# Layer 1 self-attention hands its output over by features instead of by tokens, and the dense stage behind it reads it so

## The reference

```
q = fq_sym(x @ Wq); k = fq_sym(ctx @ Wk); v = fq_sym(ctx @ Wv)     # 20 heads of 16
scores = einsum('bhnd,bhmd->bhnm', q, k) * dh ** (-0.5)
w = fq_zero(softmax(scores, axis=-1))                              # rounded to 255 levels of one global step
out = einsum('bhnm,bhmd->bhnd', w, v).transpose(0, 2, 1, 3).reshape(b, n, c)
return out @ Wo + bo
```

## Time and profile before

| what | value |
| --- | --- |
| median of 3 runs | 3719.68 us (3715.29 to 3727.21) |
| profiled execution, its own time | 3716.17 us |
| its span, first to last instruction | 3714.4 us |
| layer 1 self-attention, second block, start of the first to start of the last exponential | 2266.1 to 2564.3 us |
| the dense stage behind it | 2571.7 to about 2757 us |
| PE, DVE, ACT, POOL busy over the span | 80%, 62%, 52%, 19% |

### The profile page before, as it was taken

How to read it: one execution, slowest core, us unless ns; L and a number is a source line. 1 busy time by engine, 2 the same in 40 slices (tenths; PEclk the granted TensorE clock), 3 DMA queues, 4 the chain that set the end, 5 groups by cost and what they waited for, 6 DMA issues and landing times. The chain is left out here.

```text
span 3714.4 us, 51380 instructions
## 1 busy us (share of the span) xinstructions
PE 2975.6 (80%) x16324; PEld 1854.4 (50%) x16324; DVE 2303.9 (62%) x4118; ACT 1916.2 (52%) x3264; POOL 724.2 (19%) x1076
## 2 busy tenths in 40 slices
PE   5989999776969999979599996897750217699999
PEld 3744444464548888858111111223640104488888
DVE  4668888465533444346699996886653866344443
ACT  3438888532533323235599997996322325232322
POOL 1021111334440000000453511002330205300000
PEclk8979999887989999989555555666975559799999
DMA  6643333244730000015765436672324103201000
GB/s 182 208 143 105 104 108 105 63 117 127 184 88 18 9 17 8 0 57 153 175 156 115 114 63 88 79 98 48 89 75 152 28 11 73 45 17 32 16 23 15
DMA packets 477771, 307.04 MB, mean 83 GB/s; under 512 B 304150, under 2 KB 415982, under 8 KB 476942
## 3 DMA queue, kind: packets, MB, share of 16 engines
q1 hardware_dynamic: 471230, 288.64, 33.0%
q0 software_dynamic: 4240, 14.10, 1.3%
q10 hardware_dynamic: 2112, 1.97, 0.3%
HBM read 183.70 MB, written 118.78 MB: 81 GB/s over the span
## 5 line engine op out<-in xcount | busy, mean ns | idle before, releaser
L2053 DVE TENSOR_REDUCE neg_max<-nat 128x1 f32<-128x512 f32 x640 | 400.7, 682 | 65.0 <-PE nat L1919 64.9
L2248 PE MATMUL nat<-k_stack,q_stack 48*128 48x512 bf16 x640 | 380.7, 604 | 71.5 <-DMA k_stack<-k1w 30.8
L2282 DVE TENSOR_REDUCE m_all<-nat 128x1 f32<-128x512 f32 x640 | 423.3, 690 | 17.4 <-PE nat L2248 17.1
L2302 ACT ACTIVATE nat<-nat,m_all 128x512 f32<-128x512 f32 x640 | 427.7, 2129 | 2.3 <-DVE m_all L2282 2.3
L2302 ACT ACTIVATION_READ_ACCUMULATOR nat<-nat,m_all 128x1 f32 x640 | 403.7, 1674 | 0.0
L937 DVE SCALAR_TENSOR_TENSOR ff<-outp,bias,gel 128x512 f32<-128x512 f32 x160 | 120.1, 751 | 427.8 <-PE outp L407 427.8
L1992 ACT ACTIVATE probs<-sT 128x1024 f32<-128x1024 f32 x320 | 327.9, 1026 | 89.9 <-PE sT L1928 80.3
L2479 ACT ACTIVATE exps<-sT 128x1024 f32<-128x1024 f32 x320 | 296.3, 1083 | 15.6 <-PE sT L2419 13.7
L868 ACT ACTIVATE gel<-outp,bias 128x512 f32<-128x512 f32 x160 | 110.0, 687 | 360.6 <-PE outp L407 360.6
L749 POOL TENSOR_TENSOR rstd<-var_eps,neghalf 128x4 f32<-128x4 f32 x48 | 49.2, 1025 | 1147.6 <-DVE var_eps L919 1147.5
L872 ACT CAST ff_hi<-ff 128x512 fp32r<-128x512 f32 x160 | 99.2, 620 | 312.0 <-DVE ff L937 312.0
(11 more groups left out here) (444 smaller groups left out, 7000.5 us busy)
## 6 DMA issues: line engine op xcount, KB each, us to landing
v<-vpad SPq DMA_DIRECT2D x64, 320.0 KB, 2.8
q_stack<-q_part SPq DMA_DIRECT2D x90, 160.0 KB, 5.8
k_stack<-k1w SPq DMA_DIRECT2D x90, 160.0 KB, 10.6
q_stack<-q_hi SPq DMA_DIRECT2D x160, 64.0 KB, 2.5
k_stack<-k_hi SPq DMA_DIRECT2D x160, 64.0 KB, 2.2
v_stack<-v SPq DMA_DIRECT2D x40, 256.0 KB, 3.1
self_out<-o_nat SPq DMA_DIRECT2D x80, 128.0 KB, 2.0
attn_nat<-self_out SPq DMA_DIRECT2D x64, 160.0 KB, 2.9
```

The source lines that it names most:

```text
L2053: dve.tensor_reduce(neg_max[:, n % 2, qt, 2 * pr + ab:2 * pr + ab + 1], nat[(16 * (n + 2) + t) % 3][:, :], AX.X, ALU.max, negate=True).the ...
L2248: pe.matmul(bank[i % NAT][:, :], q_stack[half, slot, g, pr, qt * P:(qt + 1) * P], k_stack[half, slot, g, pr, :], start=True, stop=True).th ...
L2282: dve.tensor_reduce(k.m_all[:, column(i // TILES, i % TILES)], bank[i % NAT][:, :], AX.X, ALU.max, negate=True).then_inc(s["e_max_ready"], 1)
L2302: act.activation(b[:, :], b[:, :], ACT.Exp, bias=k.m_all[:, col], accum_out=k.s_all[:, col]).then_inc(s["a_nat_free"], 1)
```

## The change

The attention output stays as it lies in the bank: DVE scales o_ps straight into o_sb (two slots), SP stores the 16 rows of each of four heads by a DMA of its own, 2 KB per row, to self_out_T with features as rows. The transposes, the copy and o_nat go. The dense stage loads feature rows into attn_T by three DMAs and splits them from there: oT keeps its ACT and DVE steps, and loses PE's transposes and their banks. SP's next load waits until all three splits of the sample before are done (oT_split).

```diff
 def dense_phase(..., next_weights=(), by_feature=False):
+            attn = sb("attn_T", [P, 3, TOK]) if by_feature else sb("attn_nat", [P, TT, ZCOL])
+            n_attn = 3 if by_feature else TT + 1
 # SP
+                def load_attn_T(b, split_b=None):
+                    if split_b is not None:
+                        sp.wait_ge(s["oT_split"], at["oT_split"] + split_b * 3 + 3)
+                    src = rows(attn_in, b * D, D)
+                    sp.dma_start(attn[:, 0:2, :], src[0:2 * P].rearrange("(c p) t -> p c t", p=P)
+                                 ).then_inc(s["attn_in_loaded"], 16)
+                    for half in range(2):
+                        sp.dma_start(attn[64 * half:64 * half + 64, 2, :], src[2 * P:D]).then_inc(s["attn_in_loaded"], 16)
 # PE
-                    if kind == "oT":
+                    if kind == "oT" and not by_feature:
 # ACT (and DVE's subtraction likewise)
-                        act.copy(oT_hi[:, m, :], bank_of(st, r)[:, :]).then_inc(s["oT_hi_done"], 1)
+                        src = attn[:, m, :] if by_feature else bank_of(st, r)[:, :]
+                        act.copy(oT_hi[:, m, :], src).then_inc(s["oT_hi_done"], 1)
 def exact_self_attention
-            o_sb = sb("o_sb", [P, TOK], own=own)
-            o_nat = sb("o_nat", [P, 2, TT, 4, DH], own=own)
+            o_sb = sb("o_sb", [P, 2, TOK], own=own)
 # SP
-                            wait(sp, "a_o_normed", n - 1)
-                            sp.dma_start(rows(out, (n - 2) * TOK, TOK).rearrange("(t p) c -> p t c", p=P),
-                                         o_nat[:, n % 2].rearrange("p t h c -> p t (h c)")
-                                         ).then_inc(s[f"a_o_stored{n % 2}"], 16)
+                            wait(sp, "a_o_scaled", n - 1)
+                            for h in range(4):
+                                sp.dma_start(rows(out, (n - 2) * 64 + h * DH, DH), o_sb[VCOL * h:VCOL * h + DH, n % 2, :]
+                                             ).then_inc(s[f"a_o_stored{n % 2}"], 16)
 # PE
-                    for u in range(NU + UNITS + 1):
+                    for u in range(NU + LAG + 1):
-                        if u % UNITS == 0 and u >= 2 * UNITS:
-                            turn_output(u // UNITS - 2)
 # DVE
+                    def scale_output(n):
+                        wait(dve, "a_pv_done", TT * (n + 1))
+                        if n >= 2:
+                            wait(dve, f"a_o_stored{n % 2}", 64 * (n // 2))
+                        dve.tensor_scalar(o_sb[:, n % 2, :], o_ps[n % 2][:, :], k.out_step, None, ALU.mult
+                                          ).then_inc(s["a_o_scaled"], 1)
-                        if j == 3 and 1 <= n <= NQ:
-                            copy_output(n - 1)
-                        if j == 1 and n >= 2:
-                            norm_output(n - 2)
+                        if j == 6 and 1 <= n <= NQ:
+                            scale_output(n - 1)
```

More of the change, by code:

```diff
@@ L549, in dense_phase @@
         if main == "ff":
-            turned = {st: ("misc", n, 10) for n, st in enumerate(oT + oproj + zT)}
+            turns = ([] if by_feature else oT) + oproj + zT
+            turned = {st: ("misc", n, len(turns)) for n, st in enumerate(turns)}
         else:
             turned = {st: (st[0], st[1], n) for n, part in ((3, oT), (TT, oproj), (3, zT)) for st in part}
+            if by_feature:
+                turned = {st: x for st, x in turned.items() if st[0] != "oT"}
             if not has_o:
@@ L846, in step @@
                     if kind == "oT":
-                        bank_full(act, st, b)
+                        if not by_feature:
+                            bank_full(act, st, b)
+                        elif m == 0:
+                            act.wait_ge(s["attn_in_loaded"],
+                                        at["attn_in_loaded"] + b * (16 * n_attn) + 16 * n_attn)
                         if m == 0:
@@ L901, in step @@
                         dve.wait_ge(s["oT_hi_done"], at["oT_hi_done"] + b * 3 + m + 1)
-                        dve.tensor_tensor(oT_lo[:, m, :], bank_of(st, r)[:, :], oT_hi[:, m, :].bitcast(F32),
-                                          ALU.subtract).then_inc(s[turned[st][0] + "_drained"], 1)
+                        src = attn[:, m, :] if by_feature else bank_of(st, r)[:, :]
+                        done = "oT_split" if by_feature else turned[st][0] + "_drained"
+                        dve.tensor_tensor(oT_lo[:, m, :], src, oT_hi[:, m, :].bitcast(F32), ALU.subtract
+                                          ).then_inc(s[done], 1)
                     elif kind == "oproj":
@@ L2118, in exact_self_attention @@
             **{f"a_v_loaded{r}": 16 * BATCH // 2 for r in range(2)},
-            **{f"a_o_stored{r}": 16 * NQ // 2 for r in range(2)}}
+            **{f"a_o_stored{r}": 64 * NQ // 2 for r in range(2)}}
         at = {name: s.before(name) for name in counts}
@@ L2428, in products @@
                             if n >= 2:
-                                wait(pe, "a_o_normed", n - 1)
+                                wait(pe, "a_o_scaled", n - 1)
                         wait(pe, "e_rounded", u + 1)
@@ L2436, in products @@
                         mm.then_inc(s["a_pv_done"], 1)
-                    def turn_output(n):
-                        wait(pe, "a_o_copied", n + 1)
-                        for qt in range(TT):
-                            mm = pe.transpose(o_ps[n % 2][:, qt * P:(qt + 1) * P], o_sb[:, qt * P:(qt + 1) * P],
-                                              k.ident[:, :])
-                        mm.then_inc(s["a_o_turned"], 1)
                     wait(pe, "a_recip", 1)
```

47 lines of the change are left out of this document (22 added, 25 removed).

## The result

The changed kernel takes 3740.97 us in the median of 4 runs (3739.7 to 3745.43), the one before 3720.69 beside it (3715.29 to 3727.21): the ratio is 1.0056, 95% interval 1.0038 to 1.0074. It is slower, by about 20 us where 9 were forecast. It lies 1 us inside the range of 3711 to 3742, and outside the 3719 to 3739 that the prediction gave for its own mechanism. The profiled execution has a span of 3739.0 us.

What follows compares the result with a forecast made beforehand. Bounds: ACT's exponentials in attention, POOL's bias additions at the dense start, then a chain through z and hT_lo. 3716.17 - 5 + 15 - 3.4 + 5 = 3727.8, put at 3729 towards the runs' higher median; range 3711 to 3742.

Steps and rivals of the forecast that it cites:

- The turnings: Attention: without the transposes and copy per quad, ACT gets its scores sooner; -5 us (4 to 6).
- The late store: Attention: six scalings wait 3.2 us for a store behind the loads, ACT losing 2.5 each; +15 us (6 to 19).
- The hand-over: Attention to dense stage: earlier last scaling and shorter load let POOL's bias adds start earlier; -3.4 us (2.7 to 4).
- The steady samples: Dense stage after the start: PE's removed transposes lie beside the chain and splits from SBUF cost the same; 0 us.
- the clock: Steady dense samples: emptier PE waits longer and sometimes drops its clock; +5 us, half of 9.3.
- Rival 2: Attention: store lands in time, within 16.7 us of the loads' first issue; 3707.8, or 3712.8 with clock loss; chance 0.14.
- Rival 3: Attention: four DMAs of 16 rows land 2 us later each than one of 128; +12, 3740; chance 0.10.

Runs made afterwards that it cites:

- ring3: The changed kernel with a third o_sb slot, so a scaling waits for the store of three quads before; 3719.37 us, ratio 0.9997 to the kernel before.
- store_first: The changed kernel, still two slots, with SP issuing the store of quad n-2 ahead of the loads of quad n; 3720.31 us, ratio 0.9995 to before.
- attn_only: The changed kernel's attention with the dense stage of the kernel before, reading the new tensor by the old pattern; 3733.03 us, ratio 1.0030 to before.
- dummy_turns: The changed kernel plus twelve PE transposes of the identity per sample in the dense stage, results unread; 3734.5 us, ratio 1.0048 to before.
- ring3_bias_turns: The changed kernel with three o_sb slots, POOL's bias for two samples after the first split, others inside samples, twelve idle transposes per sample; 3714.97 us, ratio 0.9976.
- ring3_load_turn: The changed kernel with three o_sb slots, loading by features but turning tiles on PE and splitting from banks as before; 3713.42 us, ratio 0.9979.

## Why the prediction was right in kind and short in size

**The turnings, forecast -5: right.** ring3 shows 6.0 at most, the top of the range of 4 to 6. The spacing of the loads was the right view.

**The late store, forecast +15: mechanism right, size short.** Six stops of DVE came at the six places named, and ACT stopped six times behind them. The landing was right too: 19.2 to 20.5 us after the loads' first issue, 20.0 in the mean, 20.0 forecast. The term mis-sized is when the scaling is due. "The loads are issued when PE has done unit 39, so they don't move" fails: they are issued 15.7 us ahead of the rounding of unit 54 (2302.57 to 2318.23), where 16.1 were reckoned (2300.85 to 2316.95). They are tied to PE's unit 39, and PE now stands later against DVE: the first load is issued 2.86 us ahead of the rounding of unit 40 (2302.57 to 2305.43), before 3.22 (2300.85 to 2304.07). DVE's wait is 3.77 us in the mean (22.6 / 6) for 3.2. ACT gets back less of each wait than reckoned as well, 0.5 for 0.7 us, so it loses 3.3 a time for 2.5: 19.8 in all, just above the upper bound. ring3 and store_first take the wait away, wholly and nearly, by two different ways, and attn_only has it alone.

**The hand-over, forecast -3.4: the step that failed.** It was +3.6, with the wrong sign. Three parts of it, from the rows: POOL's start behind the last exponential moved from 13.1 to 11.6 us, so 1.5 and not 3.4 were gained. The first load came only 0.1 us earlier, and out_bias landed 0.55 later behind its issue (3.93 us for 3.38) and not 0.7 earlier. POOL's additions then took 2.1 us longer. And 2.94 us more came from DVE's statistics, which stand behind subtractions that had grown to 3.4 us: -1.5 + 2.1 + 2.9 = +3.5. The sentence that failed is "no row of this stage shows a source in SBUF slower than a bank". It was true of the rows, but in the steady samples POOL makes no additions to x_resid; at the one place where it does, the start, the subtractions came from a bank only. The trace of before had a sign there that I passed over, the operation ahead of POOL's power:

```profile
2596.16 2.74 DVE L919 TENSOR_SCALAR var_eps<-mv 128x4 f32<-128x4 f32 x1
```

It works on 4 elements from SBUF and takes 0.17 us in the steady samples. Here it begins 0.25 us behind one of POOL's additions (2595.91 to 2598.88), ends with it and takes 2.74. It cost nothing there, since POOL's power had to wait for the last addition anyway. I had written "POOL starts 3.4 us earlier, and since it bounds the start, so does everything" without asking whether the two engines can work at once.

The runs settle it: 689 ns from a bank beside additions, 683 from SBUF without them, 3320 from SBUF beside them. The Trainium skill (SBUF — State Buffer, section "Who interferes with whom") states that a DVE instruction with two SBUF inputs contends with a GpSimd (POOL here) instruction that reads SBUF, that DVE's one-source operations contend in their modes with two ports, and that the one that comes later is blocked for the whole of the other. These traces agree in all three: hT_lo and oT_lo are of the first kind, the rounding with its 3.24 us behaves like the second (in which mode it ran no trace shows), and each subtraction and rounding that begins within an addition ends 0.55 us behind it. It is a rule that spoke against this change, and the prediction had left it out.

**The steady samples, forecast 0 for the work and +5 for the clock: right.** They took 4.4 us longer: 5.9 more from the copy of the first to that of the eighth sample, and 1.4 less in the first, which crossed at a clock of 1.00. dummy_turns gives back 8.9. PE's wait before q0 grew to 2.34 us as forecast, but the one before zT0 stayed at 3.25 and did not grow to 3.6. In three of seven samples the copy behind q0 came 21 us behind the one before and in none 18; before, one did and two came at 18. The size is partly luck: +5 was taken as the half of a bound, and half of what came is the two quick samples of before that are gone, not a q0 at the lower clock, which alone was priced.

**Which case.** It was the forecast's, with two terms off in the same direction: +4.8 from the stores and +7.0 from the hand-over, against 11.6 forecast and 21.8 measured in the two traces. Rival 2 decided at 16.7 us to landing and the landing was at 19.2. Rival 3, the four DMAs, named a time close to the one measured, 3740. It is refuted by the landing, 19.2 to 20.5 us behind the loads' first issue, where the one DMA of before had 20.0 and 20.6: four do not land later than one. Of the range, it was the part kept for this rival that held the result, so that the number lies inside owes something to chance.

**A version that beats both.** The change by itself can't be mended by one line: ring3 is level with the kernel before, since its 6 us in the attention go again in the dense stage (203.3 us for 194.0). ring3_bias_turns is at 0.9976 (0.9963 to 0.9988) of the kernel before, some 9 us; how much of that the idle turnings bring is inside the intervals. An order that keeps POOL's additions clear of all DVE operations from SBUF, without work on PE, was not found.

## What to carry to other kernels

When a change moves an operand from a bank to SBUF, list what the other engine does at that moment, not only what the operation costs elsewhere in the trace: the same subtraction cost 0.69 or 3.3 us by POOL's company alone. A ring of two whose store stands behind a sample's loads in one queue has its slack in the landing of the loads; count it from the loads' first issue, and buy a third slot before the deadline is moved up. Work taken from an engine that waits anyway can be missed by its clock; twelve idle turnings a sample gave back 5 to 9 us in the traces of samples without additions, and 2 to 3 between the medians of those kernels.

## What was not expected of the hardware

- POOL's addition over 1280 elements (2.9 us alone) held up these DVE operations when they began within it: the 512-element subtraction with both sources in SBUF, 3.2 to 3.4 us for 0.69; the 1024-element rounding from SBUF, 3.24 for 0.69; the 4-element operation from SBUF, 2.74 for 0.17 (4.96 in ring3_load_turn, where it ended behind the second addition). It did not hold up the subtraction from a bank (0.69), the addition of a bank to x_resid (0.49) and the statistics (0.48). POOL pays too: an addition that meets a subtraction takes 3.3 us, and eight took 25.13 us against 23.02.
- Two matmuls of one row and 320 columns kept PE 0.41 us each at a granted clock of 0.50, where the steps of the product behind them, of 128 rows, follow at 0.27.
- PE did 573 matmuls in 107.5 us with the idle turnings, and 501 in 109.1 without.
